# Performer attention on Trainium2: denominators in four groups of 32 columns, inverted at half width and spread by small DMAs, with the residual rows loaded tile by tile

## The reference, cut to what matters

```python
# x: 1250 rows of 512; 8 heads of 64; pmat: 64 x 256 random features
def softmax_kernel(x, pmat):
    xp = jnp.einsum('bhnd,df->bhnf', x, pmat)
    xp = xp - jnp.max(xp, axis=-1, keepdims=True)
    return jnp.exp(xp) / math.sqrt(pmat.shape[-1])
...
kf, qf = softmax_kernel(k, pmat), softmax_kernel(q, pmat)
kv  = sum over rows of kf (x) v          # 256 x 64 for each head
out = (qf @ kv) / (qf @ sum of kf)       # numerator: 64 columns; denominator: one number
x   = x + out @ Wproj + bproj            # then layernorm and an MLP with a gelu
```

## Time and profile before

| | us |
|---|---|
| median of 3 runs | 2321.65 (2320.2 to 2322.0) |
| span of the profiled execution | 2323.9 |
| TensorE busy | 2302.6 (99% of the span) |
| VectorE busy | 1434.6 (62%) |
| GpSimd busy | 1262.3 (54%) |
| ScalarE busy | 976.5 (42%) |
| the attention's loop over steps, from the first `attend` to that of step 17 | 231.8 to 298.2 |

### The profile page before, as it was taken

How to read it: one execution, slowest core, us unless ns; L and a number is a source line. 1 busy time by engine, 2 the same in 40 slices (tenths; PEclk the granted TensorE clock), 3 DMA queues, 4 the chain that set the end, 5 groups by cost and what they waited for, 6 DMA issues and landing times. The chain is left out here.

```text
span 2323.9 us, 29585 instructions
## 1 busy us (share of the span) xinstructions
PE 2302.6 (99%) x10065; PEld 1521.8 (65%) x10065; DVE 1434.6 (62%) x2516; ACT 976.5 (42%) x1694; POOL 1262.3 (54%) x1691
## 2 busy tenths in 40 slices
PE   8999999999999999999999999999999999999999
PEld 4565655547677777777877777777767776544443
DVE  7777860523877663777674587676487766624346
ACT  4436642222666331566331376432266633312221
POOL 2005203031666892566794366796266687627775
PEclk9999999999999999999999999999999999999999
DMA  6401001330566310366310176510066621669617
GB/s 174 148 24 38 37 32 40 105 100 1 150 169 163 133 61 1 94 171 156 99 45 23 32 174 163 151 45 24 1 150 168 160 80 34 231 234 341 199 47 240
DMA packets 132356, 257.81 MB, mean 111 GB/s; under 512 B 49679, under 2 KB 51455, under 8 KB 129865
## 3 DMA queue, kind: packets, MB, share of 16 engines
q1 hardware_dynamic: 85275, 150.83, 22.0%
q0 software_dynamic: 45584, 102.75, 16.1%
q10 hardware_dynamic: 1346, 2.33, 0.4%
HBM read 213.17 MB, written 32.20 MB: 106 GB/s over the span
## 5 line engine op out<-in xcount | busy, mean ns | idle before, releaser
L118 POOL DMA_DIRECT2D cols<-w x720 | 353.4, 498 | 220.1 <-PE psum L1074 173.7
L1074 PE MATMUL psum<-cols,rows 125*128 125x256 f32 x1600 | 368.3, 379 | 0.0
L1061 PE MATMUL psum<-g_k_cols,g_q_cols 128*125 128x512 f32 (+1 forms) x960 | 360.8, 513 | 0.2
L1074 PEld LDWEIGHTS psum<-cols,rows 125*128 125x128 f32 x1600 | 303.2, 190 | 36.1
L1156 DVE CUSTOM_DVE_ANT_0 g_prob<-psum,ln_count 125x1250 f32<-125x1250 f32 x160 | 233.8, 1461 | 100.4 <-PE psum L1061 100.1
L1061 PEld LDWEIGHTS psum<-g_k_cols,g_q_cols 128*125 128x125 f32 x960 | 179.4, 187 | 165.2 <-issue 155.5
L1254 ACT ACTIVATE g_prob<-g_prob,g_row_max 125x1250 f32<-125x1250 f32 x160 | 215.8, 1348 | 122.4 <-DVE g_row_max L1156 120.3
L1170 DVE STREAM_TRANSPOSE w<-g_prob 128x1280 f32<-128x1280 f32 x160 | 241.5, 1509 | 36.7 <-DMA cols<-w 28.2
L1260 ACT ACTIVATE g_prob<-g_prob,g_row_max 125x1250 f32<-125x1250 f32 x160 | 215.5, 1347 | 69.8 <-DVE g_row_max L1145 69.5
L580 POOL TENSOR_TENSOR rows<-rows,g_bias_rows 125x512 f32<-125x512 f32 x40 | 50.0, 1271 | 186.0 <-DVE rows L570 185.9
L3358 PE MATMUL psum<-m_ew,m_x_cols 128*64 128x256 f32 (+1 forms) x576 | 150.3, 493 | 0.7 <-DMA cols<-in_L_ffn_expert_w,m_weights_of 0.7
(11 more groups left out here) (450 smaller groups left out, 4585.8 us busy)
## 6 DMA issues: line engine op xcount, KB each, us to landing
cols<-w POOLq DMA_DIRECT2D x720, 80.0 KB, 3.2
cols<-w SPq DMA_DIRECT2D x560, 80.0 KB, 3.7
w<-in_L_gnn_m_w SPq DMA_DIRECT2D x8, 1024.0 KB
slot_rows<-p_kf SPq DMA_DIRECT2D x1, 7344.0 KB, 32.9
rows<-slot_rows SPq DMA_DIRECT2D x54, 136.0 KB, 6.6
m_ew<-in_L_ffn_expert_w SPq DMA_DIRECT2D x4, 1536.0 KB, 12.4
slot_outputs<-slot_rows SPq DMA_DIRECT2D x1, 5000.0 KB
w<-in_L_mix_W SPq DMA_DIRECT2D x4, 1024.0 KB, 5.0
```

The costliest lines, as they stand in the source:

```text
L118: return eng.dma_start(out, in_, allow_slow_non_contiguous=True)
L1061: ins = pe.matmul(psum[0:P, at:at + width], q_cols[:, h, t * P:(t + 1) * P], k_cols[:, h, start:start + width], start=True, stop=True)
L1074: ins = pe.matmul(c.bank(6 + g % 2, 256).rearrange("p (u a i) -> p u a i", u=2, a=SIDE), rows[0:P, j, h * 128:(h + 1) * 128], turned_keys[ ...
```

## The change

- **TensorE.** In `attend` the four 64-column denominator matmuls (250 moving columns each) become eight with 32 stationary columns and 125 moving ones: each of head e and row tile b has its own quarter of the array's columns and of the output's partitions. They stand ahead of the four numerator matmuls, which stay as they are.
- **VectorE.** `divide` is split. `den_turned(n)` inverts 128 x 125 instead of 128 x 250. `divide(n)` now only multiplies, and waits for DMAs. In the loop `den_turned(m - 3)` and `divide(m - 4)` stand ahead of `highest(m)`; behind the loop they are woven with the projection.
- **Spreading.** `spread(eng, n, e)` issues two DMAs of 32 KB (SBUF to SBUF) that write each 32 partitions of inverses twice, to the 64 partitions of head e: SyncE for e = 0, GpSimd for e = 1.
- **Residual rows.** The one load becomes ten, one behind each of SyncE's first ten spreads. GpSimd's ten bias adds stand one ahead of each of its last ten spreads, all waiting for all ten loads.
- Semaphores for weights are shared between loads, to make room for four new ones (`den_in`); their waits ask for the same loads as before.

```diff
+        def spread(eng, n, e):
+
+            eng.wait_ge(den_made, n + 1)
+            for b in range(2):
+                r0 = (2 * e + b) * 32
+                load(eng, rden[n % 2][e * DH:(e + 1) * DH, b * P:(b + 1) * P],
+                     den_parts[n % 2][r0:r0 + 32].unsqueeze(1).broadcast_to([32, 2, P])).then_inc(den_in[n % 2][e], 16)
...
-            load(sp, x, rows_view(xn_dram[:, :])).then_inc(res_in, 16)
             w2_view = chunks(a["L0_mix_W2"])
+            for n in range(Q_STEPS):
+                spread(sp, n, 0)
+                if n < NT:
+                    load(sp, x[:, n, :], xn_dram[n * P:(n + 1) * P, :]).then_inc(res_in, 16)
...
-                for sums in range(2):
-                    at = (6 + n % 2) * BANK + sums * 2 * P
-                    for half in range(2):
-                        for e in range(2):
-                            ins = pe.matmul(psum[e * DH:(e + 1) * DH, at:at + 2 * P], kv[:, g, sums, half, e, :],
-                                            qf_cols[:, n % 2, e, half, :], start=(half == 0), stop=(half == 1))
+                at = (6 + n % 2) * BANK
+                for half in range(2):
+                    for e in range(2):
+                        for b in range(2):
+                            r0 = (2 * e + b) * 32
+                            pe.matmul(psum[r0:r0 + 32, at + 2 * P:at + 3 * P], kv[:, g, 1, half, e, 0:32],
+                                      qf_cols[:, n % 2, e, half, b * P:(b + 1) * P], start=(half == 0), stop=(half == 1),
+                                      tile_position=(0, r0))
+                for half in range(2):
+                    for e in range(2):
+                        ins = pe.matmul(psum[e * DH:(e + 1) * DH, at:at + 2 * P], kv[:, g, 0, half, e, :],
+                                        qf_cols[:, n % 2, e, half, :], start=(half == 0), stop=(half == 1))
...
-                v.reciprocal(rden, psum[0:128, at + 2 * P:at + 4 * P]).then_inc(den_made, 1)
+                v.reciprocal(den_parts[n % 2], psum[0:128, at + 2 * P:at + 3 * P]).then_inc(den_made, 1)
...
             for n in range(2, Q_STEPS):
+                if n >= 3:
+                    den_turned(n - 3)
+                if n >= 4:
+                    divide(n - 4)
                 highest(n)
-                if n >= 3:
-                    divide(n - 3)
+            den_turned(Q_STEPS - 3)
+            divide(Q_STEPS - 4)
             divide(Q_STEPS - 3)
+            den_turned(Q_STEPS - 2)
             project_dve(0)
             divide(Q_STEPS - 2)
             project_dve(1)
+            den_turned(Q_STEPS - 1)
             v.wait_ge(qf_turned, 2 * Q_STEPS)
             h_norm_dve(0)
             divide(Q_STEPS - 1)
...
-            for t in range(NT):
-                g.tensor_tensor(x[:, t, :], x[:, t, :], bias_rows[:, 1, :], ALU.add).then_inc(bp_added, 1)
+            for n in range(Q_STEPS):
+                t = n - (Q_STEPS - NT)
+                if t >= 0:
+                    g.wait_ge(res_in, 16 * NT)
+                    g.tensor_tensor(x[:, t, :], x[:, t, :], bias_rows[:, 1, :], ALU.add).then_inc(bp_added, 1)
+                spread(g, n, 1)
```

More of the change, by code:

```diff
@@ L1476, in performer @@
     out_mm, den_made, out_made = c.sems("p_out_mm", "p_den_made", "p_out_made")
+    den_in = [[c.sem(f"p_den_in{i}{e}") for e in range(2)] for i in range(2)]
     bp_added, b2_added, o_mm, o_added, h_mm, h_made = c.sems("p_bp_added", "p_b2_added", "p_o_mm", "p_o_added",
@@ L1490, in performer @@
         ones = sb("p_ones", [P, DH])
-        rden = rows[:].rearrange("p t d -> p (t d)")[:, KC * N:KC * N + 2 * P]
+        den_parts = [rows[:].rearrange("p t d -> p (t d)")[:, KC * N + i * P:KC * N + (i + 1) * P] for i in range(2)]
+        rden = [rows[:].rearrange("p t d -> p (t d)")[:, 8 * D + 2 * i * P:8 * D + 2 * (i + 1) * P] for i in range(2)]
         bias_rows = sb("p_bias_rows", [P, 4, D])
```

49 lines of the change are left out of this document (26 added, 23 removed).

## The result

The changed kernel takes 2326.47 us in the median of 20 runs (2322.09 to 2330.26); the kernel before takes 2321.89 in the median of 20 runs beside them (2319.41 to 2330.16). The ratio is 1.0016, with a 95% interval of 1.0009 to 1.0022: 2.1 to 5.1 us slower, with 3.7 in the middle (the two medians as they stand differ by 4.6). That is within 0.2%, as forecast, and the median lies inside the forecast's range of 2319.5 to 2331; but the loss is nearly three times the forecast's +1.3, and its interval reaches just beyond 0.2%.

The account below looks back on a forecast made before the run. The prediction took TensorE, busy for 99% of the span, to bound the kernel. Its terms, -4.8 in the loop, +1.7 at step 10 and +4.4 behind the loop, gave +1.3 us: 2323.0, range 2319.5 to 2331.

Parts of the forecast that it names:

- The matmuls: In the loop, four narrow tiles side by side make attend 1.56 us and an iteration 3.63: -4.8 us over 17 iterations.
- the second rival: In attend, the four tiles do not overlap fully: 2331 two at a time, 2347 one after the other; chance 0.17.
- The other engines keep 3.63: In the loop, the other engines' work fits an iteration of 3.63 us, with about 0.2 us to spare.
- L: Spread's latency from inverse to when VectorE may multiply: 2.5 to 4.35 us, taken as 3.0; up to 3.8 free in loop.
- Step 10: In the loop, GpSimd waits for the tenth load and adds a bias before spreading: +1.7 us, once (0.8 to 2.5).
- The third rival: Spreads land late, L near 4.35, by sharing engines with loads or by short rows: +8 us, 2330; chance 0.2.
- Behind the loop: After step 17's attend, waits on GpSimd's add and VectorE's order start tile 4's projection later: +4.4 us.
- the first rival: The forecast itself: four tiles side by side, L below 3.8, 2323.0; one half-speed stretch behind the loop adds 1.7; chance 0.53.
- the prediction's own signs of being wrong: Among them, behind the loop: a granted clock below 1 for longer than one stretch like that at 2060.10 to 2063.50.
- The sum: Whole kernel: -4.8 + 1.7 + 4.4 = +1.3 us, a time of 2323.0.
- the line of 4.6: Whole kernel: 4.6 us is 0.2% of its time, about what a measurement can tell from no change.

Follow-up runs that it names:

- e3: The changed kernel without its spread DMAs and VectorE's waits for them, so its numbers are not the reference's; ratio to the kernel before 1.0002.
- e10: e2 with half as many spread DMAs, tile loads behind the spreads of steps 2 to 11, and adds two at a time behind later spreads; ratio to before 0.9982.
- e6: e2 with SyncE's two spreads of a step cut in four, so that they land later; one run, first attend to step 17's 66.04 us.
- e1: The changed kernel with only GpSimd's ten bias adds moved, behind the spreads of steps 10 to 16; ratio to the kernel before 1.0004.
- e11: The changed kernel once more, without any edit; ratio to the kernel before 1.0015.
- e7: The changed kernel with three extra matmuls in TensorE's stop ahead of tile 2; one run, step 17's attend to tile 4's projection 25.87 us.
- e4: The changed kernel with six extra matmuls of TensorE, results unused, between step 19's attend and tile 2's projection; ratio to the kernel before 1.0022.
- e8: The kernel before, without any edit, run once more with a profile; span 2319.1 us, 4.8 us shorter than its first profile.
- e2: The changed kernel with the adds as in e1 and, behind the loop, VectorE's projected-tile adds ahead of step 18's inverse; ratio to the kernel before 0.9983.
- e9: e2 with half as many spread DMAs and the residual rows in one load ahead of the first spread; ratio to the kernel before 1.0049.

## Why the prediction was right, and where its sum was off

- **The matmuls**: right to the digit. `attend` 1.56, iteration 3.63; 61.66 against 66.41 where nothing stops the loop, 4.75 for the 4.8. Four tiles of 32 columns side by side run as fast as two of 64, so the second rival is out. By the factor that the prediction takes from the Trainium skill, TensorE: Matmul & The Clock Gate (Part 3, measured speedup), 2.38 for three tiles, `attend` would be 1.84. The trace does not bear that out for four: the narrow matmuls' first start to the numerators' is 0.57, which holds the change of division too.
- **The other engines keep 3.63, and L up to 3.8 is free**: right (e3, e10; e6 at 3.81). L was near the 3.0 taken where a product waited for nothing but its own spread: 318.22 - 315.32 = 2.9 for step 19. That products wait for DMAs at step 10 alone was wrong: in the loop those of steps 0, 4 and 13 waited too (1.49, 0.13, 0.19), and only the first of them cost time.
- **Step 10**: +1.7 forecast; 5.25 and 3.74 in place of 3.63 twice, +1.73. e1 removed it with the adds. That it fits to the digit is in part luck: GpSimd could add 5.8 us behind step 9's inverse (273.37 - 267.61) where the working has 5.0, and the spread came 2.4 behind the add (277.03 - 274.63) where it has 2.9.
- **The first spread**: no term stood for it. It cost 1.06 in the changed kernel, 0.95 in the second distance and 0.11 in the third (the second alone lost 0.3 to 1.3 in four more profiles). The step that failed is "I take 3.0, nearer the low end, because the queues are nearly empty in the loop", taken for every step: step 0's spread landed 5.0 behind its inverse, with the change's own tile load right behind it and a 16 KB packet of the instruction queue in its flight. The third rival named the contention with the loads, but for every step; the instruction packets, which make five spreads late even in e10, stand nowhere in the prediction.
- **Behind the loop**: +5.0 for +4.4, and +4.5 in e11. Tile 2's projection started at 15.62 (15.3 forecast) with TensorE idle ahead of it, and VectorE's chain came as worked out: counted from step 17's `attend`, tile 0 was normalised at 20.2 (20.1 forecast), step 19's product ended at 22.9 (22.8), tile 1 was normalised at 25.3 (25.2). The term that was too small is the clock's, which the sum puts at nothing and the first rival at 1.7: it kept TensorE busy until 321.69, 0.7 behind tile 1's norm, in place of waiting ahead of both transposes. Where the clock stayed at 1.00 (e7) TensorE does wait there, and tile 4 is at 25.87 for the 25.8 forecast. The stretch of 6.8 us, twice as long as the one of the earlier trace rows, is also one of the prediction's own signs of being wrong, and yet it cost only 0.5, because VectorE's chain was nearly as late.
- **The sum**: 4.75 gained, 2.8 given back in the loop, 5.0 in the tail: +3.06 against +1.3 by the profiles. The 1.06 of the first spread and the 0.6 of the tail are nearly all of the difference. The measured 3.7 (2.1 to 5.1) agrees. The forecast of no change beyond 0.2% rests on three terms that came out nearly as worked out; that 3.7 stayed under the line of 4.6 although a fourth was missing is a margin of 0.04%, and so in part luck.

**What stays open.** The ratios of e3 and e4 lie 3.3 and 3.6 us above what their distances say, beyond their intervals (e3: 84.93 - 87.77 = -2.8 for +0.5 measured, -1.6 to +2.6; e4: +1.5 for +5.1, 2.8 to 7.7); those of the other seven timed kernels, the changed one among them, lie 0.6 to 2.7 above, inside theirs. All nine on one side is much for chance, so something of about 1 us or more may be lost outside the three distances. In the profiles 0.1 to 0.6 us of it come between tile 4 and 1940 us, in all eleven edited or changed executions and not in e8, for a reason that no run shows. The rest would have to come from the stage behind or from the time before the first `attend`, which itself lies anywhere from 229.66 to 233.47; each of the two scatters by as much as is missing. No run here tells them apart. That the first spread is held by the first tile load, and longer where an instruction packet falls in its flight, fits all ten profiles with spreads, but no experiment varied either alone with enough profiles.

## What to carry to other kernels

A gain on the bounding engine is easily given back where the order of other engines' work was changed to make it: go through what stands behind every wait that the change adds, on each engine, and put work that is ready (here a projected tile's add) ahead of work that must wait. Mended in two orders, the same change is 0.17% faster (e2) in place of 0.16% slower. A DMA on whose latency an engine depends should have no large load in front of it in its queue (e9) and, as far as one profile tells (e10), none right behind it; cut the load and start it when the pipeline has slack. And leave such a DMA slack: here 3.8 us between the inverse and the product were free, and of e10's spreads all but one landed within that, the late ones too. And where the end of a program scatters by more than the effect, measure distances between marks inside one profile: they repeat to 0.01 us in an undisturbed loop.

## What the runs showed of the hardware

- Four matmuls of 32 stationary columns ran side by side: 16 records of 125 moving columns took 0.57 us to the start of the next group, the change of the array's division included, for 0.43 by four at a time and 0.14 for the change.
- Around a stop of TensorE of 2.95 us the granted clock fell to 0.50 for 6.8 us in one profile, beginning 0.9 us before TensorE resumed, and for 3.4 us in the second profile of the same kernel, beginning 0.3 us after; tile 2's projection took 6.4 and 5.2 us to the next start, for 3.5. The stop of 2.27 us in e1 had such a stretch behind it too, and that of 11.69 us in e9 (clock 0.50 from 248.7 to 252.0, 1.06 us for the narrow matmuls in place of 0.64). Behind the stop of 1.65 us in e3 the clock was 1.00.
- A load of 2500 KB ahead of a 62.5 KB spread in SyncE's queue held it to 15.9 us from issue to landing; the other half of the same spread, on GpSimd's queue, took 4.7 (e9), and both take 2.1 or 2.2 with no load about (e10, step 0).
- A packet of 16384 bytes of the instruction queue in the flight of a spread went with a landing 0.8 to 1.8 us later (e10: 3.1 to 4.1 us behind the inverse, for 2.3).
